# Attention products in batches of two steps, with sums over four key tiles and scores in three single banks

## The reference

```python
scores = jnp.einsum('bhqd,bhkd->bhqk', q, k) / math.sqrt(HEAD_DIM)     # HEAD_DIM 32, 2048 tokens
scores = jnp.where(causal[None, None, :, :], scores, jnp.float32(-1e+20))
attn = jax.nn.softmax(scores, axis=-1)
out = jnp.einsum('bhqk,bhkd->bhqd', attn, v)                            # q, k rotated; k, v shared by 4 heads
```

## Time and profile before

| | |
|---|---|
| median of three runs | 3749.15 us |
| the profiled execution | 3745.81 us |
| its span, first to last instruction | 3744.0 us |
| TensorE busy in the span | 3527.0 us (94%) |
| VectorE, ScalarE, GpSimd busy | 2269.7, 1413.4, 1638.5 us |
| chunk outputs copied by L654 | 128, the first at 808.02 us, the last at 2916.00 us |

### The profile page before, as it was taken

How to read it: one execution, slowest core, us unless ns; L and a number is a source line. 1 busy time by engine, 2 the same in 40 slices (tenths; PEclk the granted TensorE clock), 3 DMA queues, 4 the chain that set the end, 5 groups by cost and what they waited for, 6 DMA issues and landing times. The chain is left out here.

```text
span 3744.0 us, 68112 instructions
## 1 busy us (share of the span) xinstructions
PE 3527.0 (94%) x27648; PEld 2456.8 (66%) x27648; DVE 2269.7 (61%) x3912; ACT 1413.4 (38%) x1660; POOL 1638.5 (44%) x781
## 2 busy tenths in 40 slices
PE   2988888889999999999999999999999689999999
PEld 1777777756666666666666666666665278888887
DVE  3656666577676677667667666766764434444443
ACT  2222222225555555555555555555556211000000
POOL 5322222025555555555655555565566122222222
PEclk9999999979999999999999999999999799999999
DMA  9877777331221122122122112112210533434432
GB/s 247 208 195 194 191 189 191 98 79 29 59 53 36 46 56 49 35 61 51 31 55 53 46 36 57 48 37 60 51 38 15 192 71 92 98 92 91 92 95 62
DMA packets 249970, 325.82 MB, mean 87 GB/s; under 512 B 64090, under 2 KB 157914, under 8 KB 249730
## 3 DMA queue, kind: packets, MB, share of 16 engines
q1 hardware_dynamic: 231298, 255.29, 26.0%
q0 software_dynamic: 18432, 67.12, 8.1%
HBM read 223.74 MB, written 97.52 MB: 86 GB/s over the span
## 5 line engine op out<-in xcount | busy, mean ns | idle before, releaser
L678 DVE TENSOR_REDUCE mpart<-mx_ps 128x1 f32<-128x512 f32 (+3 forms) x2560 | 1432.4, 605 | 615.0 <-PE mx_ps L731 384.3
L632 POOL TENSOR_TENSOR sums<-probs 128x1024 f32<-128x1024 f32 (+1 forms) x576 | 1229.5, 2135 | 926.5 <-ACT probs L647 913.8
L647 ACT ACTIVATE probs<-st_ps 128x1024 f32<-128x1024 f32 (+1 forms) x1152 | 1063.3, 973 | 950.4 <-PE st_ps L762 687.6
L728 PE MATMUL mx_ps<-k_max,qs 96*128 96x512 f32 (+3 forms) x2560 | 907.0, 416 | 18.0 <-POOL masks L623 15.0
L762 PE MATMUL st_ps<-qs,k_score 98*128 98x512 f32 (+1 forms) x2304 | 718.8, 407 | 0.0
L728 PEld LDWEIGHTS mx_ps<-k_max,qs 96*128 96x128 f32 x2560 | 466.9, 195 | 294.8 <-DVE mpart L678 176.3
L780 PE MATMUL od_ps<-probs,vs 128*32 128x256 f32 (+1 forms) x9216 | 589.4, 373 | 0.0
L762 PEld LDWEIGHTS st_ps<-qs,k_score 98*128 98x128 f32 x2304 | 420.0, 193 | 71.1 <-issue 12.1
L780 PEld LDWEIGHTS od_ps<-probs,vs 128*32 128x32 f32 x9216 | 240.7, 109 | 226.4 <-issue 111.5
L203 POOL DMA_INDIRECT hbuf<-in_tok_table,idx x128 | 195.8, 1530 | 351.7 <-ACT xn L234 232.0
L986 POOL TENSOR_TENSOR h<-h,bb 128x1024 f32<-128x1024 f32 x32 | 105.1, 3285 | 542.1 <-DVE xn_c L1084 542.1
(11 more groups left out here) (102 smaller groups left out, 3793.6 us busy)
## 6 DMA issues: line engine op xcount, KB each, us to landing
qs<-q_hi_scratch SPq DMA_DIRECT2D x128, 256.0 KB, 4.6
h_scratch<-hbuf SPq DMA_DIRECT2D x32, 512.0 KB, 3.5
q_hi_scratch<-rot_hi SPq DMA_DIRECT2D x64, 256.0 KB
q_lo_scratch<-rot_lo SPq DMA_DIRECT2D x64, 256.0 KB
qs<-q_lo_scratch SPq DMA_DIRECT2D x64, 256.0 KB, 5.7
o_scratch<-od_sb SPq DMA_DIRECT2D x128, 128.0 KB
o_in<-o_scratch SPq DMA_DIRECT2D x32, 512.0 KB, 4.5
o_in<-recip_scratch SPq DMA_DIRECT2D x128, 128.0 KB, 7.9
```

The lines of the kernel that those rows point to most:

```text
L632: nc.gpsimd.tensor_tensor(sums[:, n % SUM_SLOTS, :, lo:QW], a, b, ALU.add).then_inc(sum_done, 1)
L647: nc.scalar.activation(probs[:, n % SLOTS, half, :, lo:QW], st_ps[:, half, :, lo:QW], ACT.Exp, scale=float(HD) ** -0.5).then_inc(exp_done, 1)
L678: nc.vector.tensor_reduce(mpart[:, h * TPC + t, kc:kc + 1], mx_ps[:, e % MAX_BANKS, 0:w], AX, ALU.max).then_inc(max_done, 1)
L728: mm = nc.tensor.matmul(out, qs[c][0:K_ROWS, h, t * P:(t + 1) * P], k_max[0:K_ROWS, kc * CT:kc * CT + w], start=True, stop=not diagonal)
```

## The change

Three things in part B:

1. The sum that GpSimd makes covers a *set*: two consecutive steps of a chunk, four key tiles (in a chunk with an odd number of steps, c even, the diagonal step is a set by itself). There are 20 sets to a group instead of 36 steps, and three additions to a set of two steps, each of which waits for the one before it.
2. `batch` is done once per set, with the values of both steps and one denominator product.
3. `st_ps` is three single banks in rotation, one for each unit, each with its own `st_ready` and its own exponential of 512 columns; the bank gained goes to `mx_ps`, which has four.

```diff
-SCORE_SLOTS, MAX_BANKS = 2, 3
+SCORE_BANKS, MAX_BANKS = 3, 4
+def sum_sets():
+    sets = []
+    for c in range(QH):
+        if c % 2 == 0:
+            sets.append((FIRST_OF[c],))
+        rest = range(FIRST_OF[c] + 1 - c % 2, LAST_OF[c] + 1)
+        sets += [(k, k + 1) for k in rest[::2]]
+    return sets
+SETS = sum_sets()
+SET_OF = [j for j, steps in enumerate(SETS) for s in steps]
...
-        st_ps = ctx.enter_context(nc.psum_tensor("st_ps", [P, SCORE_SLOTS, GROUP, QW], F32))
+        st_ps = ctx.enter_context(nc.psum_tensor("st_ps", [P, SCORE_BANKS, 2, QW], F32))
...
                 def next_v(c):
                     if not last:
-                        sp.wait_ge(batch_done, g * NS + K_LAST[c] + 1)
+                        sp.wait_ge(batch_done, g * len(SETS) + SET_OF[K_LAST[c]] + 1)
...
-            def pair_sum(g, s):
-                c, i = STEPS[s]
-                n, lo = g * NS + s, P if i == c else 0
-                pool.wait_ge(exp_done, 2 * n + 2)
-                if n >= SUM_SLOTS:
-                    pool.wait_ge(batch_done, n - SUM_SLOTS + 1)
-                a, b = (probs[:, n % SLOTS, k, :, lo:QW] for k in range(2))
-                nc.gpsimd.tensor_tensor(sums[:, n % SUM_SLOTS, :, lo:QW], a, b, ALU.add).then_inc(sum_done, 1)
+            def set_sum(g, j):
+                q = g * len(SETS) + j
+                at = sums[:, q % SUM_SLOTS]
+                diagonal = [s for s in SETS[j] if STEPS[s][0] == STEPS[s][1]]
+                wide = [(s, k) for s in SETS[j] for k in range(2) if k == 0 or s not in diagonal]
+                if q >= SUM_SLOTS:
+                    pool.wait_ge(batch_done, q - SUM_SLOTS + 1)
+                if len(wide) == 1:
+                    exp_waited(g, diagonal[0], 1)
+                    nc.gpsimd.tensor_tensor(at[:, :, P:QW], probs_of(g, diagonal[0], 0, P),
+                                            probs_of(g, diagonal[0], 1, P), ALU.add).then_inc(sum_done, 1)
+                    return
+                exp_waited(g, *wide[1])
+                step.do(nc.gpsimd.tensor_tensor(at, probs_of(g, *wide[0], 0), probs_of(g, *wide[1], 0), ALU.add))
+                exp_waited(g, *wide[2])
+                step.do(nc.gpsimd.tensor_tensor(at, at, probs_of(g, *wide[2], 0), ALU.add))
+                if diagonal:
+                    lo, last = P, (diagonal[0], 1)
+                else:
+                    lo, last = 0, wide[3]
+                exp_waited(g, *last)
+                nc.gpsimd.tensor_tensor(at[:, :, lo:QW], at[:, :, lo:QW], probs_of(g, *last, lo), ALU.add
+                                        ).then_inc(sum_done, 1)
...
-                act.wait_ge(st_ready, 2 * n + half + 1)
                 if half == 0 and n >= SLOTS:
-                    act.wait_ge(batch_done, n - SLOTS + 1)
-                nc.scalar.activation(probs[:, n % SLOTS, half, :, lo:QW], st_ps[:, half, :, lo:QW], ACT.Exp,
-                                     scale=float(HD) ** -0.5).then_inc(exp_done, 1)
+                    g_old, s_old = divmod(n - SLOTS, NS)
+                    act.wait_ge(batch_done, g_old * len(SETS) + SET_OF[s_old] + 1)
+                for h in range(0, GROUP, 2):
+                    u = 4 * n + 2 * half + h // 2
+                    act.wait_ge(st_ready, u + 1)
+                    nc.scalar.activation(probs[:, n % SLOTS, half, h:h + 2, lo:QW], st_ps[:, u % SCORE_BANKS, :, lo:QW],
+                                         ACT.Exp, scale=float(HD) ** -0.5).then_inc(exp_done, 1)
...
-                if n > 0:
-                    pe.wait_ge(exp_done, 2 * n + half - 1)
                 at = c % 2 * QW
                 for h in range(0, GROUP, 2):
-                    out = st_ps[:, half, h:h + 2, :]
+                    u = 4 * n + 2 * half + h // 2
+                    if u >= SCORE_BANKS:
+                        pe.wait_ge(exp_done, u - (SCORE_BANKS - 1))
+                    out = st_ps[:, u % SCORE_BANKS, :, :]
...
-                mm.then_inc(st_ready, 1)
+                    mm.then_inc(st_ready, 1)
...
+            def products(g, s):
+                steps = SETS[SET_OF[s]]
+                if s == steps[-1]:
+                    for k in steps:
+                        values(g, k)
+                    denominators(g, s).then_inc(batch_done, 1)
```

More of the change, by code:

```diff
@@ L499, in part_b @@
         st_ready, exp_done = sem("st_ready"), sem("exp_done")
-        sum_done, batch_done = sem("sum_done"), sem("batch_done")
+        sum_step, sum_done, batch_done = sem("sum_step"), sem("sum_done"), sem("batch_done")
         od_copied = sem("od_copied")
@@ L547, in after_scores @@
                 def after_scores(s):
-                    sp.wait_ge(st_ready, 2 * (g * NS + s + 1))
+                    sp.wait_ge(st_ready, 4 * (g * NS + s + 1))
                 def next_q(c):
@@ L623, in _, with probs_of, exp_waited @@
             nc.gpsimd.tensor_copy(masks[:], consts_in[:]).then_inc(consts_done, 1)
-            def pair_sum(g, s):
-                c, i = STEPS[s]
-                n, lo = g * NS + s, P if i == c else 0
-                pool.wait_ge(exp_done, 2 * n + 2)
-                if n >= SUM_SLOTS:
-                    pool.wait_ge(batch_done, n - SUM_SLOTS + 1)
-                a, b = (probs[:, n % SLOTS, k, :, lo:QW] for k in range(2))
-                nc.gpsimd.tensor_tensor(sums[:, n % SUM_SLOTS, :, lo:QW], a, b, ALU.add).then_inc(sum_done, 1)
+            step = Steps(pool, sum_step, 0)
+            def probs_of(g, s, k, lo):
+                return probs[:, (g * NS + s) % SLOTS, k, :, lo:QW]
+            def exp_waited(g, s, k):
+                pool.wait_ge(exp_done, 4 * (g * NS + s) + 2 * k + 2)
+            def set_sum(g, j):
[21 more added lines that the diff above has]
+                                        ).then_inc(sum_done, 1)
             for g in range(GROUPS):
-                for s in range(NS):
-                    pair_sum(g, s)
+                for j in range(len(SETS)):
+                    set_sum(g, j)
         @block.scalar
@@ L785, in denominators @@
                 c, i = STEPS[s]
-                n, lo = g * NS + s, P if i == c else 0
-                pe.wait_ge(sum_done, n + 1)
+                n, j = g * NS + s, SET_OF[s]
+                q = g * len(SETS) + j
+                lo = P if SETS[j] == (s,) else 0
+                pe.wait_ge(sum_done, q + 1)
                 if lo:
@@ L793, in denominators @@
                     mm = nc.tensor.matmul(od_ps[h * HD:(h + 1) * HD, 1, lo:QW], ones[:],
-                                          sums[:, n % SUM_SLOTS, h, lo:QW], start=False, stop=s in LAST_OF)
-                mm.then_inc(batch_done, 1)
+                                          sums[:, q % SUM_SLOTS, h, lo:QW], start=False, stop=s in LAST_OF)
+                return mm
+            def products(g, s):
[4 more added lines that the diff above has]
+                    denominators(g, s).then_inc(batch_done, 1)
             def batch(g, s):
                 if s >= 0:
-                    values(g, s)
-                    denominators(g, s)
+                    products(g, s)
                 elif g > 0:
-                    values(g - 1, s + NS)
-                    denominators(g - 1, s + NS)
+                    products(g - 1, s + NS)
             def group(g, first, last):
@@ L823, in _ @@
             for s in range(NS - LAG, NS):
-                pe.wait_ge(exp_done, 2 * ((GROUPS - 1) * NS + s + 1))
+                pe.wait_ge(exp_done, 4 * ((GROUPS - 1) * NS + s + 1))
                 batch(GROUPS - 1, s)
```

2 lines of the change are left out of this document (1 added, 1 removed).

## The result

The changed kernel takes **3791.18 us** (median of four runs, 3786.72 to 3800.42) against 3748.27 us for the kernel before on the same chip: ratio 1.0118, 95% interval 1.0098 to 1.0137. It is 1.2% slower. 3753 was forecast, as a trade that cancels (3735 to 3775 for that case), in a range of 3695 to 3802 over all cases. The profiled execution took 3790.73 us, its span is 3788.9, 44.9 us more than the 3744.0 of before.

The account below looks back on a forecast made before the run. TensorE was taken to bound steady groups. Fifteen groups at 11.1 - 11.7 give -9, group 0 -4, last group +16.6: +3.6 on 3744.0, plus 1.8 outside the span and 3.3 to the median, 3753 us; range 3695 to 3802.

Parts of the forecast that it names:

- a trade that cancels: Main case: per group, stalls of 11.1 us against 11.7 saved on batches; 3735 to 3775 us, chance 0.5.
- ScalarE as the bound: Rival: exponentials don't overlap and bound the 16 steps per group without a batch; 3784 or 3832 us, chance 0.16.
- the increments: Rival: 72 more `st_ready` increments per group serialise at about 26 ns each; 30 us longer, 3783, chance 0.03.
- GpSimd in every group: Rival: GpSimd's dependent additions, or the `qs` load, bind every group; 3765 to 3800 us, chance 0.06 for both.
- denominators and entries saved: TensorE, batches 36 to 20: 16 denominators (0.44) and 16 batch entries (0.29) go, 11.7 us less per group.
- The wait at the fourth unit: Unit 4 of each step waits for unit 1's exponential to free its bank, a 1.18 us chain; 11.1 us per group.
- Nothing for turns: Turns counted only as some 0.04 us between the halves of three steps; no wait of a turn was priced.
- VectorE and the fourth bank: Maxima in pairs of steps without a batch between: the fourth bank holds what is left, no stall, 0.
- Group 0: First group, steps with 6 or more entries: fourth bank and shorter TensorE work give back 0 to 10 us, 4 taken.
- Last group: From step 18 on, without maxima, GpSimd's additions set the time: 49.8 becomes 66.4, 16.6 us lost, bounds 12 to 20.
- hidden stalls: Rival: hand-over is nothing and weight loads are fetched ahead of the wait; 3684 to 3735 us, chance 0.24.
- set sums don't shorten the stream: Rival: a batch's entry cost grows with its length, so sets save nothing; 3800 us and more, chance 0.01.

Follow-up runs that it names:

- one_step_sets: Changed kernel with sets of one step, so 36 batches per group, keeping three score and four maxima banks: 3949.4 us, ratio 1.0543.
- sb3_mb3: Changed kernel with three banks for the maxima in place of four, one PSUM bank left unused: 3894.9 us, ratio 1.0397.
- between_sb4: Changed kernel with four score and three maxima banks, and one maximum instead of two at either end of a step: 3705.4 us, ratio 0.9886.
- late_turn: Changed kernel with the lone transpose of step 17 moved from between the halves to behind the last unit: 3787.0 us, ratio 1.0101.
- sb4_mb3: Changed kernel with four single score banks and three for the maxima in place of three and four: 3710.8 us, ratio 0.9901.
- sets_old_scores: Kernel before with only the sets added; scores, 1024-column exponentials and banks as before: 3714.1 us, ratio 0.9913.
- more_between: Changed kernel with one maximum instead of two at either end of a step, so more stand between its halves: 3620.9 us, ratio 0.9658.

## Why the prediction was right and wrong

**Right in mechanism, wrong in the sizes that had to cancel.** In a trade of -11.7 against +11.1 a term that is off by 13% is the whole result. The measured 3791 lies inside the range of 3695 to 3802, but outside the 3735 to 3775 that the prediction gave to the case that came true. What kept it inside was the room made for ScalarE as the bound, the increments and GpSimd in every group, none of which happened: that is luck. And one of its own signs of being wrong came up: waits for `probs` above 14 us per group; the weight loads waited 15.5 (161.1 / 10.4). Step by step:

1. *TensorE bounds the steady group, denominators and entries saved: -11.7.* Right, with about 11.4 measured: 10.9 between one_step_sets and after, and 0.55 for the turn.
2. *The wait at the fourth unit: +11.1.* The step that was mis-sized: 12.6 measured (one_step_sets). The place was right, 28 stalls per group, and the chain had the right links. (Between the halves the code puts a full-width maximum in six full steps and a narrow one in six, not seven and five; the sum stays 11.1.) It was 1.245 us long instead of 1.18: the exponential starts 0.49 after unit 1, where 0.43 was read from the earlier trace rows, a pair of units of which only the second was waited for. With 28 stalls that is 28 x 0.065 = 1.8 us; 1.5 were found. The bounds (6.5 and 16.5) held it.
3. *The units that follow are not stalled.* Right. The last row of the stall's timeline is the fourth unit again, of the diagonal step behind, without an entry between its halves: its load waits 0.33 us there, where 0.42 of stall was forecast.
4. *Nothing for turns.* Wrong: +0.55 per group (0.85 of wait, less the stall of step 17's fourth unit that it covers). With steps shortened the transpose of step 17 comes before VectorE has made `mcol`. The prediction asked what is late next only of units and maxima.
5. *VectorE and the fourth bank: 0 in a steady group.* Right as it stands: the weight loads of maxima wait for `mpart` 15.9 us in 10.4 groups, about four in five of them behind a batch; before it was 93.0 in 9 groups. The runs add what that zero hides: without the bank it would have been 6.2 us per group. "The fourth bank holds what is left while the long batch runs" is what sb3_mb3 and between_sb4 show.
6. *Group 0: -4 more.* Wrong: group 0 is 0.5 slower, so beyond a steady group's +1.7 it gained 1.2. A part is the clock: from 854.5 to 857.5 us it is 0.50, and late_turn, without such a stretch, takes 144.3 for group 0, of which the turn explains 0.3. Why the rest of the 4 did not come stays open.
7. *Last group: +16.6.* 19.1 measured, within the bounds of 12 to 20. GpSimd takes 7.22 us per full set, where 7.3 was forecast. But the sum had only GpSimd there; the stall at the fourth unit, with no maxima between the halves from step 18 on, was left out, and alone it makes the last group 14.6 longer (one_step_sets). The two overlap in time, so the number came close all the same.
8. *SyncE and the `qs` load: 0; exponentials 0.49 apart; increments 0.* Right. Four exponentials take 2.06 us, sb4_mb3 is no slower than sets_old_scores, and more_between leaves no room for the increments.

The sum, against the forecast of +3.6 in the span: the -9 and -4 of the first 15 groups became +26.6 (26.1 and 0.5), the last group's +16.6 became +19.1, and what lies before and behind gave 0.8 back. Of the 2.5 us per group between -0.6 and +1.9, 1.5 are step 2, 0.5 to 0.6 step 4, 0.3 step 1, and 0.2 the few longer periods.

The rivals: hidden stalls fell with the 28 waits per group; ScalarE and increments with more_between; GpSimd per group with its 17 us of idle time before L663, the `qs` load with the absence of any wait of TensorE for a DMA; "set sums don't shorten the stream" with one_step_sets.

## What to carry to other kernels

When a bank is taken from one rotation and given to another, price both on the same step: the wait is (producer to consumer, consumer's length, hand-over back) minus what stands between the two uses, and it can be filled by moving independent work between them instead of buying a bank. Here two more maxima between the halves were worth 11.0 us per group, about as much as all the batches saved. Where waits overlap, as the turn's and the fourth unit's did, or GpSimd's and the banks' in the last group, taking one away uncovers the other: price them together. And a forecast that is the difference of two equal terms should be given with the error of each, since the sign hangs on a tenth of either.

## What the runs showed of the hardware that was not expected

- ScalarE's first exponential starts 0.49 us after the start of the 512-column matmul that feeds it, where 0.43 was read from a pair; the whole bank hand-over matmul, exponential, next matmul is 1.245 us.
- Two additions of GpSimd that depend on each other start 2.44 to 2.46 us apart, at 2.37 to 2.38 busy; where the next does not depend on the one before, 2.32.
- A releaser in brackets is not yet a cost. The first weight load behind a batch starts 0.41 us late in both kernels; with three banks the trace puts it down to VectorE, with four to the issue itself. Before, from its timeline:

```profile
1040.61 0.19 PEld L728 LDWEIGHTS mx_ps<-k_max,qs 96*128 96x128 f32 x1 [0.41 <-DVE mpart L678]
```

and after, at the same place behind a batch:

```profile
1203.41 0.30 PEld L771 LDWEIGHTS mx_ps<-k_max,qs 96*128 96x128 f32 x2 [0.41 <-issue]
```

  So such waits, 198 of the 279 of before, cost it little or nothing at that place, while the same label in the middle of a run of maxima in sb4_mb3 went with a real delay, seen in the matmuls' starts.
